# Later places in the GpSimd queue for the attention and LSTM weight loads of a fused attention + recurrent kernel

## What is computed

```python
x = x + LN(attn(LN(x)))              # Wq Wk Wv Wo, bias bo; q, k, v as (n, head, row, 64)
#   att = softmax(einsum('nqhd,nkhd->nhqk', q, k) / 8): for each row among its 16 heads
x = x + LN(ffn(LN(x)))
# ffn: a scan over the first axis, 8 steps, 4096 rows each (512 of them on a core)
f = sigmoid(x_t @ wf.T + c @ uf.T + bf)
i = sigmoid(x_t @ wi.T + c @ ui.T + bi)
g = tanh(x_t @ wc.T + c @ uc.T + bc)
c = f * c + i * g                    # in sequence over t
h = tanh(x @ wo.T + c_final @ uo.T + bo)
```

## Time and profile before

| | |
|---|---|
| two timed runs | 3444.03 and 3612.59 us, median 3528.31 us |
| the profiled execution | 3428.84 us |
| its span, slowest core (core 5) | 3427.2 us |
| spans of the eight cores | 3406.1 to 3427.2 us |
| TensorE (PE) matmuls busy | 1959.6 us, 57% |
| VectorE (DVE) / ScalarE (ACT) busy | 1013.6 us, 30% / 554.1 us, 16% |
| weight loads of PE (PEld) / GpSimd (POOL) | 935.7 us, 27% / 333.5 us, 10% |
| DMA, mean over the span | 55 GB/s, 186.96 MB |

### The profile page before, as it was taken

The page is one execution under the profiler, slowest core; times in us unless marked ns, Lnnn a source line. Parts: engine busy times, 40 slices in busy tenths (PEclk is TensorE's granted clock), DMA queues, the critical chain, the costliest instruction groups (busy, mean ns, idle before and its releaser), DMA issues.

```text
span 3427.2 us, 31730 instructions; the slowest of 8 cores (3406.1 to 3427.2 us)
## 1 busy us (share of the span) xinstructions
PE 1959.6 (57%) x9540; PEld 935.7 (27%) x9540; DVE 1013.6 (30%) x1754; ACT 554.1 (16%) x1257; POOL 333.5 (10%) x510
## 2 busy tenths in 40 slices
PE   1666555554555555454544023999999996886000
PEld 0333222222322223232222011444444442332000
DVE  0434333343333433343333022212211211222222
ACT  1011111112112111212122022111111110111000
POOL 1000010101111010111111110000000001101111
PEclk9766666666666666666655556999999998999555
DMA  7011121212212121222222824000000004111333
GB/s 120 30 39 33 36 57 45 66 55 57 63 55 56 51 67 54 64 56 57 55 64 70 138 74 101 1 13 13 13 11 2 13 13 68 28 31 49 126 127 112
DMA packets 167403, 186.96 MB, mean 55 GB/s; under 512 B 109886, under 2 KB 122174, under 8 KB 167230
## 3 DMA queue, kind: packets, MB, share of 16 engines
q0 software_dynamic: 53456, 151.38, 17.3%
q1 hardware_dynamic: 113792, 33.57, 4.1%
HBM read 151.68 MB, written 58.72 MB: 61 GB/s over the span
## 4 chain that ended last, share of the span: by engine, by line
PE 54%; DVE 16%; DMA 9%; issue 8%; ACT 6%; another core or an unknown queue 4%; DVEq 1%; POOL 1%; ACTq 0%; POOLq 0%; SPq 0%
PE ps_p L1650 12%; PE ps_a L2036 10%; PE ps_a L2042 10%; DMA xin<-x 5%; PE ps_p L1446 5%; PE ps_p L2129 3%; PE ps_p L2136 3%; DVE otn L1821 3%; DVE qst L1719 2%; DMA vst<-v_scr 2%; PE ps_rl L1805 2%; ACT pt_sb L1784 2%; PE ps_a L1772 2%; PE ps_ot L1805 2%
## 5 line engine op out<-in xcount | busy, mean ns | idle before, releaser
L1784 ACT ACTIVATE pt_sb<-ps_a 128x512 bf16<-128x512 f32 x128 | 76.1, 594 | 1112.5 <-PE ps_a L1772 1112.5
L2056 ACT ACTIVATE gat<-ps_a,biases 128x512 f32<-128x512 f32 x192 | 132.0, 687 | 582.1 <-PE ps_a L2042 582.1
L1805 PE MATMUL ps_ot<-pt_sb,vst 128*65 128x128 bf16 x256 | 60.4, 256 | 289.0 <-DMA vst<-v_scr 241.1
L2066 DVE TENSOR_TENSOR cT<-cT,gat 128x512 f32<-128x512 f32 x64 | 44.3, 692 | 577.0 <-ACT gat L2056 577.0
L1446 PE MATMUL ps_p<-wo_sb,zlT_t 128*128 128x512 bf16 x512 | 176.9, 521 | 48.6 <-DVE zlT_t L1432 48.6
L1650 PE MATMUL ps_p<-wq_sb,xlnT_t 128*128 128x512 bf16 x512 | 185.1, 541 | 33.5 <-DVE xlnT_t L1636 33.5
L2036 PE MATMUL ps_a<-xtT_sl,wq_sb 128*128 128x512 bf16 x512 | 133.6, 408 | 48.5 <-DVE zb L2019 33.7
L2129 PE MATMUL ps_p<-qst,gat 128*128 128x512 bf16 x512 | 122.9, 383 | 59.2 <-DMA gat<-xt_scr 33.8
L2042 PE MATMUL ps_a<-zb,wk_sb 128*128 128x512 bf16 x512 | 125.7, 390 | 0.0
L2136 PE MATMUL ps_p<-kst,zb 128*128 128x512 bf16 x512 | 121.3, 380 | 0.0
L2042 PE MATMUL ps_a<-zb,wo_sb 128*128 128x512 bf16 x512 | 121.0, 379 | 0.0
(11 more groups left out here) (159 smaller groups left out, 2741.7 us busy)
## 6 DMA issues: line engine op xcount, KB each, us to landing
xin<-x POOLq DMA_DIRECT2D x96, 512.0 KB, 4.5
xin<-xr POOLq DMA_DIRECT2D x32, 512.0 KB, 4.3
x<-x1t POOLq DMA_DIRECT2D x32, 512.0 KB, 3.1
out<-x1t POOLq DMA_DIRECT2D x32, 512.0 KB, 3.0
v_scr<-vtok SPq DMA_DIRECT2D x32, 256.0 KB, 2.0
vst<-v_scr POOLq DMA_DIRECT2D x128, 64.0 KB, 3.5
od<-orow SPq DMA_DIRECT2D x128, 64.0 KB, 1.8
zin<-od POOLq DMA_DIRECT2D x128, 64.0 KB, 3.5
```

Source lines behind the costliest of these rows:

```text
L1784: ch_exp.inc(sc.activation(pt_sb[:, gbuf * 512:(gbuf + 1) * 512], ps_a[:, abank * 512:(abank + 1) * 512], AF.Exp, scale=0.125))
L1805: inst = t.matmul(psot[0:65, pk4 * 128:(pk4 + 1) * 128], vst[:, vslot * 260 + pk4 * 65: vslot * 260 + (pk4 + 1) * 65], pt_sb[:, gbuf * 512 ...
L2056: ch_gev.inc(sc.activation(gat[:, gi * 512:(gi + 1) * 512], ps_a[:, pg * 512:(pg + 1) * 512], func, bias=biases[:, bcol + mt:bcol + mt + 1]))
```

## The change

Two edits. At the start, the four weights leave `g_consts`, so that `CONSTS` counts the seven small constants alone. Wq, Wk, Wv get a function of their own, put down on POOL's list behind the x loads of tiles 0 and 1, with a semaphore `ch_aw1` that every projection matmul group waits for; Wo gets another, behind the x load of tile 2, with `ch_aw2`, that the matmuls with Wo wait for. At the tail, the four `emit_P2` and eight `emit_LN3` of block 7 are put down ahead of `g_fc1` and `g_fc2` and no longer behind them. What is computed and what is transferred stays the same.

```diff
         ch_cd.inc(g.dma_start(out=kst[64:73, :], in_=maskk[:]))
-        for w_sb_, wdram in ((wq_sb, wqT), (wk_sb, wkT), (wv_sb, wvT),
-                             (wo_sb, woT)):
-            ch_cd.inc(g.dma_start(
+    P("gpsimd", g_consts)
+    ch_cd.bump(7)
+    CONSTS = ch_cd.n
+    ch_aw1 = c("aw1", 16)
+    ch_aw2 = c("aw2", 16)
+    WQKV_RDY = 3 * 16
+    WO_RDY = 16
+
+    def g_wqkv(g):
+        for w_sb_, wdram in ((wq_sb, wqT), (wk_sb, wkT), (wv_sb, wvT)):
+            ch_aw1.inc(g.dma_start(
                 out=w_sb_[:].rearrange("p (ft m) -> p ft m", ft=8),
                 in_=wdram.rearrange("(ft p) m -> p ft m", p=128)))
-    P("gpsimd", g_consts)
-    ch_cd.bump(11)
-    CONSTS = ch_cd.n
+
+    def g_wo(g):
+        ch_aw2.inc(g.dma_start(
+            out=wo_sb[:].rearrange("p (ft m) -> p ft m", ft=8),
+            in_=woT.rearrange("(ft p) m -> p ft m", p=128)))
...
             def f_zmm(t, zt_=zt_, fc=fc, psp=psp, zrdy=ZT_RDY,
                       pf=psfree[fc], bob=BOB):
+                t.wait_ge(ch_aw2.sem, WO_RDY)
...
                           xrdy=XT_RDY, pf=psfree[fc]):
+                    t.wait_ge(ch_aw1.sem, WQKV_RDY)
...
     emit_P1_front(0, 0)
     emit_P1_front(0, 1)
+    P("gpsimd", g_wqkv)
+    ch_aw1.bump(3)
     emit_P1_qtr(0, 0)
     emit_P1_front(0, 2)
+    P("gpsimd", g_wo)
+    ch_aw2.bump(1)
...
+    emit_P2(B - 1, 0, ODS_hist[B - 1])
+    emit_LN3(24)
...
+    emit_P2(B - 1, 3, ODS_hist[B - 1])
+    for tt in range(27, 32):
+        emit_LN3(tt)
+
     A_PJ = ch_pj.n
     A_AM = ch_am.n
...
     P("gpsimd", g_fc2)
     ch_cd.bump(2)
 
-    emit_P2(B - 1, 0, ODS_hist[B - 1])
-    emit_LN3(24)
...
-    emit_P2(B - 1, 3, ODS_hist[B - 1])
-    for tt in range(27, 32):
-        emit_LN3(tt)
```

## The result

The changed kernel takes 3427.11 us (median of 38 runs, 3396.51 to 3613.84), the kernel before 3444.92 us (37 runs, 3421.11 to 3665.84). The ratio is 0.994, 95% interval 0.9925 to 0.9955: 0.6% less time, some 21 us, between 15 and 26. The prediction had 3406 against a profiled execution of 3428.84, a ratio of 0.9934, with a range of 3385 to 3520 and 0.93 for within 2%. Both kernels have executions that are 1 to 6.5% longer, which the ratio leaves out (the median of two runs that stood beside the kernel before held one of these).

The account below looks back on a forecast made before the run. The prediction took two idle stretches behind weight loads, 60.97 us at the start and 83.00 us at 1886 us, to bound the kernel. 3428.84 - 24.6 (start) + 2.0 (tail) gave 3406 us, range 3385 to 3520.

Parts of the forecast that it names:

- What bounds the kernel: No engine works for 60.97 us at the start and 83.00 us at 1886 us; both were laid to weight loads.
- The start: First projection matmul waits for Wv and starts at 51.6 instead of 76.18 us, 24.6 us earlier (bounds 23.1 to 25.1).
- the two x tiles: At the start, x loads now ahead of the weights delay Wv's landing by 2.5 us for both, from 48.9 to 51.4.
- Nothing else in the start is late: Wo lands near 65 us with no one waiting; tile 3's x load comes at 67.3; the rest shifts by 24.6 us.
- The tail: Block 7's P2 starts 69.6 us earlier, but the scan's weights come later; first gate matmul 2119.4 against 2117.36, 2.0 us later.
- SP's transfers: Ahead of the scan, two stores (1.14 us each) and two input slices (7.4 us) delay the weights by 9.7 us.
- The sum: Whole kernel: 3428.84 - 24.6 + 2.0 = 3406 us, 0.7% below the profiled execution.
- Free or starved slices: Rival ahead of the scan: SP's transfers cost the weights nothing (3397 us) or wait for them (3399 us); chance 0.2.
- Weights slowed by 12.5 us for each of SP's four transfers: Rival ahead of the scan: the weights lose 4 x 12.5 us, kernel ends 17.7 us later than before, 3447; chance 0.08.
- Only Wo's share at the start: Rival at the start: x tiles or constants come too late to hide the 14.1 us chain; only 13 us go, 3418; chance 0.08.
- The tail's 70 us stay won: Rival at the tail: weights load beside P2 and LN3, so the 69.6 us stay gained, 3335 us; chance 0.03.

Follow-up runs that it names:

- semaphore-split kernel: Kernel before, same order of issues, but the small constants, Wq/Wk/Wv and Wo count on separate semaphores; x loads still behind the weights; ratio 0.997.
- slices-last kernel: Changed kernel, but SP loads the scan's first two input slices only after all scan weights have landed; ratio 0.9913 to the kernel before.
- kernel with the gaps: Changed kernel, but five scan weights and the bias vectors are issued while POOL waits in P2 of blocks 6 and 7, ui last; 3348.22 us, ratio 0.9732.

## Why the prediction was right, point by point

**What bounds the kernel.** Two stretches without any work, both of them weight loads at the head of POOL's list. The first of them shrank by the landing of Wo and the norm chain, the second moved; both as read from the chain and the landings.

**The start.** Predicted: constants at 12.0, chain done at 26.1, Wv at 51.4, first matmul at 51.6, 24.6 us gained. The profile of after: 11.97, 25.9, 52.4, 52.65. On eight cores the mean gain is 23.9 us (76.3 to 52.4), inside the bounds of 23.1 to 25.1. Wv landed a microsecond late in the profiled core, but most of that is the choice of core: over eight cores it landed at 49.4 before and at 52.2 after, so the two x tiles and the later issue cost 2.7 us where 2.5 were taken, and the profiled core of the kernel before, at 48.9, was among its quickest. The prediction came to the 2.5 by calling an x tile a quarter of a weight; in bytes read it is an eighth (0.52 of 4.19 MB), and an eighth of 12.5 us, twice, is 3.1. The semaphore-split kernel shows the norm, transpose and evacuation of the first tile by themselves, 6.6 us (63.63 to 70.23).

By the Trainium skill ("DMA: Bandwidth & Descriptors", Specifications) two x tiles would be an estimated 2.9 us at 358 GB/s; against the measured 2.7 it is as near as the 2.5 that was taken.

**Nothing else in the start is late.** Wo was issued at 24.98 and landed 41.1 us later, at 66.1 (predicted near 65). The x load of tile 3 was issued at 68.06 (67.3). No one waited for Wo. That the gain reaches the end is shown by the kernel with the start only, 0.9931.

**The tail.** Predicted: P2 69.6 us earlier, weights issued at its end, 81.1 us for six, 9.7 on it for SP's transfers, 5.65 for the state, in sum 2.0 us longer. Measured: P2 of block 7 begins 70.2 us earlier (13.1 us behind the last Wo matmul, 83.3 before), 92.1 us from wf's issue to ui's landing against 90.8 predicted, 2102.7 to 2108.5 for the state, and 233.0 us for the whole stretch, which the prediction put at 233. That this number is met to the microsecond is partly luck: wf was issued 134.9 us behind the last Wo matmul, 1.9 sooner than the predicted 136.8, and the weights took 1.3 us longer. Over eight cores the stretch is 4.0 us longer (233.9 to 237.9) in the changed kernel and 2.9 in the one with the tail only, not 2.0. The term that is mis-sized is SP's: the slices were put at 7.4 us from the share of the engines they used in the old trace, and cost 9.2 (9.5 over the cores). The share of busy engines served here as the measure, and was a little low.

**The sum.** -23.9 at the start, +4.0 at the tail: -19.9 us, where the ratio says -20.7 (15 to 26) and the prediction -22.6. These are the two stages that the edits reach. The profiled executions as wholes don't show it: attention was 2.9 us longer and the part behind the gate 7.6, which leaves 9.4 us of gain in the mean of the eight spans; both parts differ by as much or more between kernels that don't touch them. What bears the sum is the ratios: 0.9931 for the start alone, 0.9992 for the tail alone, 0.994 for both.

**The rivals.** Free or starved slices: out, by the slices-last kernel. Weights slowed by 12.5 us for each of SP's four transfers, with a slower kernel: out, all four cost 11.0 (92.1 less the predicted 81.1 without them; the slices' share of it is measured, the stores' is not). Only Wo's share at the start: out, the norm chain was done 26.5 us ahead of the landing of Wv. The tail's 70 us stay won: out as long as POOL's order puts the weights last, and the kernel with the gaps shows what that rival was worth once the order allows it: 71 us of the stretch (233.0 to 162.3).

The Trainium skill's rule of turns between queues ("DMA: Bandwidth & Descriptors", Queues, rings and completion order), which the prediction weighed against starving, agrees with the run: the slices landed amid the weights, each late, and the weights were late by 9.2 us, where the engine time of the slices had been put at 7.4.

## What to carry to other kernels

Moving a bulk load from ahead of a dependent chain to behind it moves the stall and doesn't remove it, unless something else runs while the load does; what removes it is a place in the queue where the issuing engine waits anyway and the load's whole duration fits. Here the buffers of five of the six weights were free early enough for such places, three from the last projection on and two from the last scores, and each load took 16 to 20 us there. Hiding these five took the kernel from a ratio of 0.994 to 0.9732, 2.1%, where reordering the tail gave nothing. At the start, a small load that heads a long chain goes ahead of the big ones and counts on a semaphore of its own: the semaphore alone gave 6 us, both together 24.

## What the runs showed of the hardware that was not expected

Two 1 MB slices, issued together, landed 5.4 and 7.8 us after their issue when nothing ran beside them, and 24.4 and 40.1 us after it beside the weight loads, while the weights lost only 9.2 us to the two of them: the small transfers pay far more for the sharing than the large ones. And after each idle of 5.6 to 8.1 us the 16 matmuls of 128x512 took 4.9 to 6.5 us in the kernel where each projection waits for its own weight, against 3.62 in a run of them, so a matmul burst split to follow its loads is paid for at each piece. The length of the idle doesn't decide it alone. Behind 27.78 us without work the first burst took 5.04 us, at a granted clock that the profile gives as 1.00; behind a short transpose and 1.05 us of idle, the second tile's first burst took 3.61 us on some cores of the changed kernel and up to 6.12 on others.
